# First expert layer of a four-layer kernel: ranks and picks in bf16, weights fetched with the rows, keys' weights folded, shared expert moved behind the picks

## The reference, cut to what matters

```python
h = x.reshape(-1, Hd)                                   # 1024 x 256, after a layer norm
scores = jnp.sqrt(jax.nn.softplus(h @ gate_w.T))        # 1024 x 32
_, topk_idx = jax.lax.top_k(scores + bias[None, :], K)  # K = 6
topk_w = jnp.take_along_axis(scores, topk_idx, axis=1)
topk_w = topk_w / jnp.sum(topk_w, axis=-1, keepdims=True) * SCALE      # 1.5
onehot = jax.nn.one_hot(topk_idx.reshape(-1), E)
pos = jnp.cumsum(onehot, axis=0) - 1                    # a token's place in its expert
valid = pos < CAP                                       # CAP = 96
inter = jax.nn.silu(g) * u                              # g, u: the expert's rows times w_gate, w_up
yb = inter @ w_down                                     # added to the token's row with its weight
si = jnp.clip(jax.nn.silu(h @ sg.T) * (h @ su.T), -10, 10)
return routed + si @ sd.T                               # the shared expert takes all tokens

# second layer, attention
kv_c = kv @ W_kvc                                       # 256 x 64
q_nope = (q_c @ W_uq); k_nope = (kv_c @ W_uk)           # 16 heads of 128
scores = (q_nope . k_nope + q_rope . k_rope) * scale
```

## Time and profile before

| | us |
|---|---|
| median of 3 runs (lowest to highest) | 1341.39 (1340.81 to 1342.95) |
| profiled execution, its own time | 1340.05 |
| span of its trace | 1338.7 |
| busy: PE / DVE / ACT / POOL | 1098.2 / 825.2 / 618.3 / 523.9 |
| mean granted TensorE clock | 0.872 |

### The profile page before, as it was taken

How to read it: one execution, slowest core, us unless ns; L and a number is a source line. 1 busy time by engine, 2 the same in 40 slices (tenths; PEclk the granted TensorE clock), 3 DMA queues, 4 the chain that set the end, 5 groups by cost and what they waited for, 6 DMA issues and landing times.

```text
span 1338.7 us, 18730 instructions
## 1 busy us (share of the span) xinstructions
PE 1098.2 (82%) x6259; PEld 869.7 (65%) x6259; DVE 825.2 (62%) x2048; ACT 618.3 (46%) x1729; POOL 523.9 (39%) x570
## 2 busy tenths in 40 slices
PE   5898788277965995469999999999996597795895
PEld 2537544135655784469888898898985366474783
DVE  3666422075555787767787777887775656465443
ACT  1531244101121223368797887978874131363253
POOL 1300277444542453335445344454431054131453
PEclk9955799778996998669999999999997669797897
DMA  9200288700000002001101010010000250003294
GB/s 367 96 1 0 80 202 197 193 1 0 0 13 12 12 1 114 32 1 49 39 11 48 1 48 20 29 49 1 17 1 1 76 142 1 0 1 142 82 348 150
DMA packets 42688, 86.39 MB, mean 65 GB/s; under 512 B 8160, under 2 KB 26624, under 8 KB 40928
## 3 DMA queue, kind: packets, MB, share of 16 engines
q1 hardware_dynamic: 35216, 72.72, 15.9%
q0 software_dynamic: 7376, 12.48, 4.2%
HBM read 67.24 MB, written 17.94 MB: 64 GB/s over the span
## 4 chain that ended last, share of the span: by engine, by line
PE 54%; DVE 17%; issue 10%; POOL 9%; ACT 5%; DMA 5%; SPq 0%; DVEq 0%; POOLq 0%; ACTq 0%
PE bank L186 29%; PE bank L195 7%; PE bank L2263 3%; DVE a_qn L2416 2%; DMA sum<-f_ys,f_index 2%; PE bank L1181 2%; PE bank L2252 2%; POOL a_qk_rstd L234 2%; POOL f_got L1044 2%; POOL sum L1052 1%; DVE a_catw L2051 1%; PE bank L388 1%; DVE f_pick L932 1%; POOL a_q_rstd L234 1%; PE bank L382 1%
## 5 line engine op out<-in xcount | busy, mean ns | idle before, releaser
L2714 POOL TENSOR_TENSOR a_p<-a_p,a_tot 128x128 f32<-128x128 f32 x64 | 52.1, 832 | 210.0 <-DVE a_tot L2387 210.0
L981 ACT ACTIVATE swi_gated<-bank 128x128 f32<-128x128 f32 (+1 forms) x87 | 24.0, 276 | 126.6 <-PE bank L186 126.4
L2438 DVE TENSOR_REDUCE a_top<-bank 128x2 f32<-128x512 f32 (+1 forms) x96 | 57.7, 603 | 35.9 <-PE bank L2263 22.3
L186 PE MATMUL bank<-a_proj_high,a_catq 128*128 128x256 f32 x256 | 69.5, 305 | 12.0 <-DVE a_catq L2057 9.0
L2655 ACT ACTIVATE a_cat<-bank,a_ismooth 128x256 bf16<-128x256 f32 x128 | 50.3, 482 | 49.9 <-PE bank L2298 49.9
L1044 POOL DMA_INDIRECT f_got<-h_rows,f_index x32 | 30.2, 943 | 101.7 <-DVE f_index L952 90.2
L2416 DVE TENSOR_SCALAR a_qn<-bank,a_qk_minus,a_qk_rstd 128x128 f32<-128x128 f32 x192 | 64.1, 403 | 5.4 <-issue 2.7
L186 PE MATMUL bank<-a_proj_low,a_catq 128*128 128x256 f32 x256 | 67.4, 297 | 0.0
L2583 ACT ACTIVATE a_qn<-bank,a_q_shift,a_q_rstd 128x128 f32<-128x128 f32 x128 | 48.3, 460 | 40.6 <-POOL a_q_shift L237 40.6
L2263 PE MATMUL bank<-a_kt,a_qt 128*128 128x256 f32 x256 | 65.0, 399 | 0.0
L195 PE MATMUL bank<-const,rows 128*128 128x128 f32 x96 | 20.2, 398 | 53.9 <-POOL rows L280 35.9
(11 more groups left out here) (447 smaller groups left out, 3587.5 us busy)
## 6 DMA issues: line engine op xcount, KB each, us to landing
expert<-in_experts SPq DMA_DIRECT2D x42, 384.0 KB, 3.8
f_expert<-in_experts SPq DMA_DIRECT2D x23, 384.0 KB, 6.5
a_raw_w<-in_groups SPq DMA_DIRECT2D x8, 1024.0 KB, 5.9
a_raw_proj<-in_groups SPq DMA_DIRECT2D x8, 512.0 KB, 3.9
f_xs<-l_zero SPq DMA_DIRECT2D x1, 3999.0 KB, 21.4
l_expert<-in_experts SPq DMA_DIRECT2D x10, 384.0 KB, 7.8
f_got<-f_xs SPq DMA_DIRECT2D x6, 516.0 KB, 7.6
l_weights<-in_l SPq DMA_DIRECT2D x1, 2784.0 KB, 22.0
```

What stands on the lines that cost most here:

```text
L186: ins = pe.matmul(out, lhs, rhs, start=start and n == 0, stop=stop and n == len(pairs) - 1, skip_group_check=shared)
L2438: v.tensor_reduce(top[:, cs], src, AX.X, ALU.max, negate=True).then_inc(*s["top_ready"].one())
L2714: g_.tensor_tensor(cross_probs(m, ti), cross_probs(m, ti), over(m.tot[n % 2][:, first:first + HPG], SC), ALU.mult).then_inc(*s["cross_weig ...
```

## The change: what it does

- *Keys*: the products of the two weight matrices of each head, which need no token, are taken first (16 of 64x96, L387), in four banks, copied by ScalarE in four operations into `fold` (it borrows the tile of the shared expert's result), and then multiplied with kv_c (16 of 96x256, L396), two heads to a bank and to a copy. `uk` is laid out 128 x (16 x 64) for it.
- *Mask*: choices in bf16, each compared for all tiles at once, then 6 summed as 3 + 3, 1 + 1, 1 + 1 instead of one reduction.
- *Ranks*: one triangular product over all tiles and seven with ones, each adding a tile's mask to all later tiles, in bf16; no running sums. The place is (rank + 1) x mask.
- *Picks*: places, counts (1..96, written out by GpSimd once as 96 x 32) and picks are bf16 with the 32 experts innermost, so an expert's 96 columns of a weight load lie 64 bytes apart. Two columns of facts instead of 32 x 5.
- *Weights* are written to memory as 32 more columns of `h_rows` (SP, a DMA of its own, waited for by GpSimd) and come with the gathered row; 1152 bytes a row. Six gather buffers instead of four; a gather also waits for the VectorE product that reads the weight of the buffer's last user.
- *Shared expert*: behind all picks and the index, in TensorE's and VectorE's programs.

```diff
-    for r in range(H1 + 2):
-        if r < H1:
-            on.wait_ge(*s["knope_copied"].at(r - 1))
-            pe.matmul(k.bank[6 + r % 2][:, 0:CTX], uk[:, r, :], k.kvc[:], start=True,
-                      stop=True).then_inc(*s["knope_made"].one())
...
+    for n, bank in enumerate(KEY_BANKS):
+        on.wait_ge(*banks_free[n])
+        for i in range(FOLD):
+            ins = pe.matmul(k.bank[bank][0:KVC, i * QC:(i + 1) * QC], uk[:, n * FOLD + i, :], uq[:, n * FOLD + i, :],
+                            start=True, stop=True)
+        ins.then_inc(*s["fold_made"].one())
+    for n in range(H1 // 2):
...
+            ins = pe.matmul(bank[0:QC, i * CTX:(i + 1) * CTX], fold[:, h * QC:(h + 1) * QC], k.kvc[:], start=True,
+                            stop=True)
```

```diff
 # layer0_ffn_sync
+    on.wait_ge(*s["weights_ready"].at(1))
+    q.dma_start(m.h_rows[0:TOK, D:D + E0].rearrange("(t p) e -> p t e", p=P), m.weight[:]).then_inc(
+        *s["h_rows_out"].one())
 # layer0_ffn_tensor
-    for i in range(NT):
-        ins = products(pe, k.bank[5][:, i * E0:(i + 1) * E0], [(k.c["before"], m.route.mask[:, i, :]),
-                                                               (k.c["ones"], m.before[:, i, :])])
+    pe.matmul(k.bank[4][:, 0:NT * E0], m.before[:], m.mask[:], start=True, stop=False, skip_group_check=True)
+    for i in range(NT - 1):
+        ins = pe.matmul(k.bank[4][:, (i + 1) * E0:NT * E0], m.ones[:],
+                        under(m.mask[:, i * E0:(i + 1) * E0], NT - 1 - i), start=False, stop=i == NT - 2,
+                        skip_group_check=True)
...
+            ins = pe.matmul(k.bank[6][0:CAP, 2 * x:2 * x + 2], m.picks[r % 2][:, :, x], m.facts[:, r, :],
+                            start=r == 0 and x == 0, stop=r == NT - 1, skip_group_check=True)
...
-                ins = pe.matmul(k.bank[6][0:CAP, x * 5:(x + 1) * 5], m.picks[r % 2][:, x, :], m.facts[:, r, x, :],
-                                start=r == 0 and x == 0, stop=r == NT - 1, skip_group_check=True)
 # layer0_ffn_vector
+    for n in range(K0):
+        ins = v.tensor_tensor(m.hits[:, n, :].rearrange("p (t e) -> p t e", t=NT), over(m.where_f[:, :, n], E0),
+                              under(c["iota_e"], NT), ALU.is_equal)
+    v.tensor_tensor(m.hits[:, 0:3, :], m.hits[:, 0:3, :], m.hits[:, 3:6, :], ALU.add).then_inc(*step.one())
...
-        v.tensor_tensor(m.picks[i % 2][:], over(m.place[:, i, :], CAP), under(c["iota_c"], E0),
-                        ALU.is_equal).then_inc(*s["pick_ready"].one())
+        v.tensor_tensor(m.picks[i % 2][:], under(m.place[:, i, :], CAP), m.counts[:], ALU.is_equal).then_inc(
+            *s["pick_ready"].one())
...
-            v.scalar_tensor_tensor(m.inner[n % 3][0:CAP, :], k.bank[n % 3][0:CAP, I:2 * I], m.slot_w[:, x:x + 1],
+            v.scalar_tensor_tensor(m.inner[n % 3][0:CAP, :], k.bank[n % 3][0:CAP, I:2 * I], m.got[x % DEEP_GOT][:, D + x:D + x + 1],
 # layer0_ffn_pool
+    g.tensor_scalar(m.counts[:], over(k.c["iota_c"], E0), 1.0, 0.0, ALU.add, ALU.add).then_inc(*s["counted"].one())
     on.wait_ge(*s["indexed"].at(1))
-    on.wait_ge(*s["h_rows_out"].at(2))
+    on.wait_ge(*s["h_rows_out"].at(3))
     for r in range(E0 + 5):
         if r < E0:
-            on.wait_ge(*s["got_flipped"].at(r - DEEP + 1))
+            on.wait_ge(*s["got_flipped"].at(r - DEEP_GOT + 1))
+            on.wait_ge(*s["swi_inner"].at(NT + r - DEEP_GOT + 1 if r >= DEEP_GOT else 0))
```

More of the change, by code:

```diff
@@ L709, in layer0_ffn @@
         m.t["size"] = m.t["scores"]
-        m.route = Route(k, scope, E0, K0)
+        m.best = sb("f0_best", [P, NT, 8])
+        m.where = sb("f0_where", [P, NT, 8], U32)
+        m.where_f = sb("f0_where_f", [P, NT, 8], BF16)
+        m.hits = sb("f0_hits", [P, K0, NT * E0], BF16)
+        m.mask = sb("f0_mask", [P, NT * E0], BF16)
+        m.before, m.ones = sb("f0_before", [P, P], BF16), sb("f0_ones", [P, P], BF16)
         k.vhead = [sb(f"a1_vhead{n}", [P, CTX]) for n in range(3)]
@@ L714, in layer0_ffn @@
         m.total = sb("f0_total", [P, NT])
[L715 to L719, removed]
+        m.place = sb("f0_place", [P, NT, E0], BF16)
+        m.facts = sb("f0_facts", [P, NT, 2], BF16)
+        m.counts = sb("f0_counts", [P, CAP, E0], BF16)
+        m.picks = [sb(f"f0_pick{n}", [P, CAP, E0], BF16) for n in range(2)]
         m.gated = [sb(f"swi_gated{n}", [P, I]) for n in range(3)]
@@ L795, in layer0_ffn_tensor @@
     on.wait_ge(*came)
[L796 removed]
+    on.wait_ge(*s["place_ready"].at(1))
     for r in range(NT + 2):
@@ L899, in layer0_ffn_vector @@
     on.wait_ge(*step.now())
[L900 to L909, removed]
@@ L910, in layer0_ffn_vector @@
-    on.wait_ge(*step.now())
+    v.tensor_tensor(m.weight[:], m.weight[:], over(m.total[:], E0), ALU.mult).then_inc(*s["weights_ready"].one())
     on.wait_ge(*s["place_made"].at(1))
-    v.tensor_tensor(flat_t(m.place), flat_t(m.place), k.bank[5][:, 0:NT * E0], ALU.add).then_inc(
+    v.scalar_tensor_tensor(flat_t(m.place), k.bank[4][:, 0:NT * E0], 1.0, m.mask[:], ALU.add, ALU.mult).then_inc(
         *s["place_ready"].one())
-    on.wait_ge(*s["facts_set"].at(1))
-    facts, rest, weight = m.facts, m.rest, m.weight
@@ L917, in layer0_ffn_vector @@
[L917 to L921, removed]
-    on.wait_ge(*step.now())
-    v.tensor_copy(facts[:, :, :, 3], rest[:]).then_inc(*step.one())
-    on.wait_ge(*step.now())
-    v.tensor_tensor(rest[:], rest[:], facts[:, :, :, 3], ALU.subtract).then_inc(*step.one())
@@ new lines, in layer0_ffn_vector @@
+    on.wait_ge(*s["picked"].at(NT))
+    table = m.table
+    v.tensor_copy(table[:].rearrange("p e f -> p (e f)"), k.bank[6][0:CAP, 0:E0 * 2]).then_inc(*step.one())
+    on.wait_ge(*step.now())
+    v.tensor_tensor(m.number[:], table[:, :, 0], table[:, :, 1], ALU.add).then_inc(*step.one())
+    on.wait_ge(*step.now())
+    v.tensor_scalar(m.empty[:], m.number[:], 0.0, c["slot1"][0:CAP, :], ALU.is_equal, ALU.mult).then_inc(*step.one())
+    on.wait_ge(*step.now())
+    v.scalar_tensor_tensor(m.index[:], m.number[:], -1.0, m.empty[:], ALU.add, ALU.add).then_inc(*s["indexed"].one())
@@ L934, in layer0_ffn_vector @@
+    for i in range(NT):
         on.wait_ge(*s["swi_gated"].at(i + 1))
```

149 lines of the change are left out of this document (71 added, 78 removed).

## The result

| | before | after |
|---|---|---|
| median of the runs side by side, us | 1341.10 (8 runs) | 1331.89 (8 runs) |
| profiled execution: span / own time, us | 1338.7 / 1340.05 | 1329.0 / 1330.74 |
| granted TensorE clock, mean | 0.872 | 0.871 |
| first gather / first scatter / last scatter | 148.66 / 163.58 / 255.84 | 133.04 / 152.83 / 245.48 |

The ratio is 0.9936, 95% interval 0.9917 to 0.9956: 9.2 us faster, where 27.4 were forecast. The first scatter comes 10.75 us earlier, the last 10.36, the span ends 9.7 earlier. So the place was right (the start of the loop decides, the loop keeps its pace of 3.0 us), and the amount was not.

The account below looks back on a forecast made before the run. Routing up to GpSimd's first scatter, then GpSimd's loop, was taken as the bound. Its terms put the first scatter at 136.2 instead of 163.58, loop unchanged: -27.4 us, 1312.7 profiled, 1314 as median; range 1306 to 1334.

Parts of the forecast that it names:

- Start of the stage: ScalarE's two folded-block copies before its logarithm make VectorE's step behind it 0.6 us later, bounds 0.2 and 1.0.
- Mask: VectorE's routing mask takes 3.35 us instead of 5.0, a gain of 1.65, and is ready at 85.8.
- Picks, VectorE: VectorE's bf16 operation for each of eight picks takes 1.76 us instead of 3.36.
- rival 2: VectorE's picks stay at 3.36 us because one operand repeats along the middle dimension: +7, so 1321; chance 0.09.
- Picks, TensorE: Weight loads with small matmuls stay at 84 ns, 2.69 us a tile at low clock; last pick ends at 111.4.
- rival 1: TensorE's strided weight loads in the picks are slow, 146 to 163 ns each: +16 to +20, 1330 to 1334; chance 0.34.
- Shared expert: Alone behind the picks from 111.4, two rounds at low clock and six at high, ending at 129.1.
- the last part: From the end of the shared expert to the first scatter: 7 us estimated, bounds 5 and 10.7.
- Loop: GpSimd's gathers and scatters keep their pace of 3.0 us; the extra bytes a row cost 0.
- rival 4: Wider gathered rows cost GpSimd more in the loop; a doubled gather makes 31 us, so 1345; chance 0.05.
- The first four chances: Forecast 0.45, rival 1 0.34, rival 2 0.09, Rival 3 0.07; given as 0.94 for faster by over 2.7 us.
- Rival 3: The clock rises early in the picks and a tile takes VectorE's 1.8 us: 7 less, 1307; chance 0.07.

Follow-up runs that it names:

- small-counts kernel: Changed kernel with counts kept as 192 values that VectorE repeats, in place of 3072: 1344.3 us beside 1342.5 of the changed kernel on that chip.
- the adjoining layout: Changed kernel with experts outermost in the picks, so a weight load reads adjoining columns: 1320.6 us, ratio 0.9851 to the kernel before.

## Why the prediction was wrong, step by step

The first step needs one line of VectorE's timeline before, the addition behind the exponential:

```profile
66.38 0.29 DVE L862 TENSOR_SCALAR f_one_plus<-f_small 128x256 f32<-128x256 f32 x1 [2.21 <-ACT f_small L992]
```

- *Start of the stage.* +0.6 forecast, +0.63 measured (69.08), and that is luck, since three shifts stand in it. VectorE's addition behind the exponential starts 0.55 us earlier (65.83 instead of 66.38), for a reason that was not looked for. ScalarE's two copies of 0.42 us cost 0.47 (the wait for the logarithm is 2.25 us in the small-counts kernel, 1.78 in the earlier trace rows). GpSimd's 10.56 us operation on the counts costs 0.7: from the addition's start to the step behind the logarithm it is 3.25 us, and 2.55 in the small-counts kernel. The prediction put that operation at nothing, since it lies within GpSimd's idle time; but VectorE's addition of 0.29 us ran until 68.52, 0.14 after that operation's end at 68.38.
- *Mask.* 85.8 forecast, 85.73 measured. *Keys* off the path: shown by undoing them. *Ranks* under the weight operations, first pick at 88.1 forecast, 87.91 measured.
- *Picks, VectorE.* 1.76 us forecast and measured; rival 2 is out here, and is what the adjoining layout does.
- *Picks, TensorE.* This is the step that failed: "I take the lower one, since its row is the same instruction on the same engine". The load costs 163.6 ns, within a nanosecond of the upper bound. 8 x (5.23 - 2.69) = 20.3 us, and the picks end at 131.8 instead of 111.4. The argument against rival 1 was that 0.87 ns a column at the low clock "may hide part of a slower read". That is so in part, and it saved nothing: a strided load takes 164 ns at either clock, 1.7 ns a column, and not 0.65 more than an adjoining one, so the slower read alone sets the pace. The same instruction with another access pattern was not the nearest row; a row with a like pattern was, though from another engine. That VectorE's 1.69 ns an element gave the number so closely is partly luck, as 16 bytes apart cost 177 ns.
- *Index.* 1.3 us from the last pick to the first gather (131.76 to 133.04), 1.4 forecast; the weights' transfer was hidden.
- *Shared expert.* 17.7 us forecast, 14.3 measured: the clock rose within two rounds, but the rounds at the high clock are 1.4 us (139.75 to 141.16), not 1.66. With the last part as estimated (7 us), the first scatter came 21.0 us behind the picks, not 24.8.
- *Loop.* 3.0 us a round, gathers at 0.94 us with 1152 bytes a row: rival 4 is out. The last scatter came 10.36 earlier.

So the sum of the measured terms: 27.4, less the 20.4 by which the picks end late, and 3.8 more behind them (24.8 - 21.0), is 10.8, the 10.75 of the first scatter. Rival 1, at 1330 to 1334, is what happened; the chances were 0.34 for it and 0.45 for the forecast. (The first four chances add up to 0.95, not 0.94.) Rival 3 (the clock rises in the picks) would not even have helped, since these loads don't follow the clock.

## What to carry to other kernels

When an operand is laid out anew for the engine that writes it, price every engine that reads it, by a row with the same stride. Here a layout in pairs, 4 bytes between the columns, served both: VectorE's double rate and TensorE's full pace, some 30 us below the kernel before in place of 9. And an engine's idle time is free only for what doesn't block a neighbour: GpSimd's long operation held up a short one of VectorE.

## What the runs showed of the hardware

- A weight load of 96 bf16 columns, with its matmul of 2 columns, takes 80 ns with columns 4 bytes apart, 90 with 8, 177 with 16 and 164 with 64, at a granted clock of 0.50. With 64 bytes and a matmul of 5 columns it takes 164 (5.26 / 32) at granted clocks of 0.50 and of 1.00, where adjoining columns take 84 and 49 (2.69 / 32 and 1.57 / 32). That 16 bytes cost more than 64 was not explained.
- A bf16 compare of 3072 elements on VectorE takes 1.76 us when an operand repeats along an outer dimension (also as runs of two values) and 3.35 us when it repeats along the innermost.
- An fp32 addition of 256 elements on VectorE, 0.29 us, took 2.69 beside a GpSimd operation and ended 0.14 us after it; VectorE's copy of the logits from a bank, in the same stretch (63.20), took 0.42 as before. The Trainium skill (SBUF — State Buffer, SBUF: two separate sides) has the two engines share a pair of ports, which some of their operations hold for a whole instruction; the trace agrees.
